# Two-layer graph network on one core: drains for own-semaphore waits, index loads for two bodies at a time, four places for edge loads

## The reference

```
h = relu(layernorm(x))
# layer 0
m    = relu(concat(h[src], edge) @ Wmsg.T + b)
m    = relu(m @ Wmsg2.T + b2)
mean = segment_sum(m, dst) / count
x    = x + concat(h, mean) @ Wapply.T + b
# layer 1
h     = relu(layernorm(x))
alpha = softmax of edge_weight over the edges of one dst
agg   = normalise(segment_sum(alpha * h[src], dst))
comb  = normalise(0.5 * (h @ Wself + b + agg @ Wnb + b))
out   = x + layernorm(comb) * gamma + beta
```

## Time and profile before

| | us |
|---|---|
| median of three runs | 10865.57 |
| the profiled execution | 10872.07 |
| its span in the trace | 10870.3 |
| POOL busy | 6155.9 (57%) |
| PE busy | 5331.9 (49%) |
| DVE busy | 3580.0 (33%) |
| ACT busy | 1136.7 (10%) |

### The profile page before, as it was taken

The page is one execution under the profiler, slowest core; times in us unless marked ns, Lnnn a source line. Parts: engine busy times, 40 slices in busy tenths (PEclk is TensorE's granted clock), DMA queues, the critical chain, the costliest instruction groups (busy, mean ns, idle before and its releaser), DMA issues.

```text
span 10870.3 us, 94616 instructions
## 1 busy us (share of the span) xinstructions
PE 5331.9 (49%) x26549; PEld 4117.8 (38%) x26549; DVE 3580.0 (33%) x14159; ACT 1136.7 (10%) x2108; POOL 6155.9 (57%) x6486
## 2 busy tenths in 40 slices
PE   4666666666655555566666533332333233233334
PEld 3444444444444344344444423222222222222224
DVE  4333233323222222222222433333333333333336
ACT  2111111111111111111111200000000000000002
POOL 4555555555554444455555466666666666666663
PEclk7777777777777677777777655655555555555556
DMA  4222222222222222222222222221111111111112
GB/s 151 56 57 54 56 56 55 57 58 57 61 67 56 57 57 59 58 55 56 58 56 57 65 57 56 56 55 49 46 46 47 46 46 47 46 46 47 46 47 72
DMA packets 412673, 618.83 MB, mean 57 GB/s; under 512 B 171795, under 2 KB 274175, under 8 KB 411263
## 3 DMA queue, kind: packets, MB, share of 16 engines
q0 software_dynamic: 206336, 422.99, 15.0%
q1 hardware_dynamic: 192624, 183.30, 6.1%
q10 hardware_dynamic: 13200, 6.56, 0.2%
HBM read 576.45 MB, written 35.92 MB: 56 GB/s over the span
## 4 chain that ended last, share of the span: by engine, by line
another core or an unknown queue 49%; PE 25%; issue 12%; DVE 12%; ACT 1%; DVEq 1%; DMA 0%; SPq 0%; POOL 0%; ACTq 0%; POOLq 0%
PE bank L1056 13%; DVE acc L884 7%; PE bank L1118 6%; PE bank L1115 3%; PE bank L1053 2%; DVE onehot L887 1%; DVE work L887 1%; ACT work L581 1%; DVEq L866 1%; DVEq L884 0%; DVE xq L711 0%; DVE acc L711 0%; DVE acc L995 0%; ACT work L587 0%
## 5 line engine op out<-in xcount | busy, mean ns | idle before, releaser
L493 POOL DMA_INDIRECT rows_ring<-p_table,idx x3224 | 3087.5, 958 | 2951.8 <-DMA idx<-in_src_ring 1790.9
L884 DVE TENSOR_TENSOR acc<-acc,bank 128x128 f32 x6448 | 1826.0, 283 | 7192.7 <-remote 5639.5
L493 POOL DMA_INDIRECT rows_ring<-h_table,idx x3224 | 3052.5, 947 | 1635.2 <-issue 1013.2
L887 DVE TENSOR_SCALAR onehot<-iota,dloc,coef 128x128 f32<-128x128 f32 x4840 | 1703.6, 355 | 16.5 <-ACT coef L558 13.3
L1056 PE MATMUL bank<-work,rows_ring 128*128 128x128 f32 x3216 | 694.6, 370 | 1867.6 <-DVE work L887 665.6
L1056 PE MATMUL bank<-onehot,work 128*128 128x128 f32 x6448 | 1094.4, 325 | 863.4 <-issue 676.4
L1056 PE MATMUL bank<-onehot,rows_ring 128*128 128x128 f32 x3232 | 743.8, 401 | 1247.1 <-remote 594.9
L1056 PEld LDWEIGHTS bank<-work,rows_ring 128*128 128x128 f32 x3216 | 597.9, 270 | 1968.7 <-issue 1911.4
L1056 PEld LDWEIGHTS bank<-onehot,work 128*128 128x128 f32 x6448 | 1002.8, 237 | 898.9 <-issue 711.3
L1056 PEld LDWEIGHTS bank<-onehot,rows_ring 128*128 128x128 f32 x3232 | 651.6, 297 | 1323.7 <-issue 1261.4
L1118 PE MATMUL bank<-work,we_sb 64*128 64x512 f32 x1612 | 1045.4, 724 | 164.7 <-issue 164.1
(11 more groups left out here) (121 smaller groups left out, 1066.1 us busy)
## 6 DMA issues: line engine op xcount, KB each, us to landing
work<-in_edge_t SPq DMA_DIRECT2D x403, 256.0 KB
rows_ring<-p_table,idx POOLq DMA_INDIRECT x3224
rows_ring<-h_table,idx POOLq DMA_INDIRECT x3224
idx<-in_src_ring SPq DMA_DIRECT2D x404, 8.0 KB
ht_rows<-rows_ring SPq DMA_DIRECT2D x25, 256.0 KB, 2.3
p_table<-rows_ring SPq DMA_DIRECT2D x25, 256.0 KB, 2.5
work<-ht_rows SPq DMA_DIRECT2D x25, 256.0 KB
h_table<-work ACTq DMA_DIRECT2D x25, 256.0 KB
```

The costliest lines, as they stand in the source:

```text
L493: pool.indirect_dma_start(out=rows_ring[:, 16 * h + G * k + j, :], out_offset=None, in_=table[:, :], in_offset=bass.IndirectOffsetOnAxis(a ...
L884: dve.tensor_tensor(win, win, ps_sum[layer][k % slots][:, j * P:(j + 1) * P], ALU.add).then_inc(added, 1)
L887: ins = dve.tensor_scalar(hot_slots[layer][k % slots][:, j * P:(j + 1) * P], iota[:, :], dloc[:, ds(t, 1)], coef[:, ds(t, 1)], ALU.is_equa ...
```

## The change

1. **Drains.** `Order` is gone. `link` is now a `dve.drain()` behind the instruction; in `tail_step` the marks become drains, on ACT too. Before each addition into `acc` stands a drain in place of the wait at L882, and the semaphore of the sums is raised once a group, at its fourth addition, in place of four times. PE's and ACT's waits on it count groups (`FINAL` is rounded up to groups).
2. **Indices.** `idx` holds two pairs of bodies, 64 tiles each. A load brings 64 tiles, 102 loads in all in place of 404. In layer 0, SP loads the pair for bodies i+2 and i+3 when PE has done the m1t steps of bodies up to i-1; in layer 1 alike. POOL waits for indices once in two bodies.
3. **Edges.** `ef_ring` has four places, on both halves of the partitions (`we_sb` is held twice to match). The load of a chunk waits for the group six before its first. `load_pre` comes at the end of a body's loads.

```
-                        if later(gs * G + j):
-                            dve.wait_ge(added, gs * G + j)
+                        dve.drain()
                         win = acc[:, ds(at[j], P)]
-                        dve.tensor_tensor(win, win, ps_sum[layer][k % slots][:, j * P:(j + 1) * P], ALU.add).then_inc(added, 1)
+                        total = dve.tensor_tensor(win, win, ps_sum[layer][k % slots][:, j * P:(j + 1) * P], ALU.add)
...
+                if adds:
+                    total.then_inc(added, 1)
...
-                for h in range(2):
-                    if h and beside is not None:
-                        load_pre(beside)
-                    half = 2 * i + h
-                    if later(i):
-                        load_idx(0, half, h, i)
-                    for c in range(2):
-                        chunk = 2 * half + c
...
-                        if later(chunk, 2):
-                            sp.wait_ge(S["m1t_in_psum"], 2 * chunk - 2)
+                for chunk in range(4 * i, min(4 * i + 4, -(-NG // 2))):
+                    if chunk >= 4:
+                        sp.wait_ge(S["m1t_in_psum"], 2 * chunk - 6)
+                    sp.dma_start(ef_ring[chunk % 4], edge_t[chunk, :, :]).then_inc(S2["edges_loaded"][chunk % 4], 16)
+                if i >= 2 and i % 2 == 0 and i // 2 + 1 < NPAIR:
+                    sp.wait_ge(S["m1t_in_psum"], 8 * i)
+                    load_idx(0, i // 2 + 1)
+                if beside is not None:
+                    load_pre(beside)
...
+            def next_idx(i):
+                if i >= 2 and i % 2 == 0 and i // 2 + 1 < NPAIR:
+                    sp.wait_ge(S["sums1_in_psum"], 8 * i)
+                    load_idx(1, i // 2 + 1)
...
+                if i % 2 == 0:
+                    pool.wait_ge(s_idx[layer][turn], 16 * (pair // 2) + 16)
                 for h in range(2):
-
-                    pool.wait_ge(s_idx[layer][h], 16 * i + 16)
...
-            order = Order(dve, S["vector_order"])
-            link = order.link
+
+            def link(ins):
+
+                dve.drain()
```

More of the change, by code:

```diff
@@ L45 @@
 PARTS = 8
-FINAL = [min(T, (E - N + (c + 1) * G * P - 1) // P + 1) for c in range(NBATCH)]
-X1_AT = -(-FINAL[0] // G) + 3
+FINAL = [-(-min(T, (E - N + (c + 1) * G * P - 1) // P + 1) // G) for c in range(NBATCH)]
+X1_AT = FINAL[0] + 3
 LAST_BODIES = X1_AT // 8
@@ L146, in gnn @@
         wgt = work[:, 10 * 512:10 * 512 + LEN]
-        ef_ring, m1t_sb, m2_sb = work[0:DE, 0:2048], place[6:8], place[8:10]
+        m1t_sb, m2_sb = place[6:8], place[8:10]
+        ef_ring = [work[DE * (n // 2):DE * (n // 2) + DE, 1024 * (n % 2):1024 * (n % 2) + 1024] for n in range(4)]
         ring4 = [rows_ring[:, 4 * n:4 * n + 4, :] for n in range(6)]
@@ L346, in stage_scalars, with load_idx @@
                 sp.dma_start(stage[0:T - whole * P, whole, :], coef_flat[n][whole * P * P:EP].rearrange("(t e) -> t e", e=P)).then_inc(S["scalars_staged"], 16)
[L348 to L351, removed]
+            def load_idx(layer, pair):
+                h = (pair + layer) % 2
+                sp.dma_start(idx[:, h, :], src_ring[pair, :, :]).then_inc(s_idx[layer][h], 16)
             def loads0(i):
@@ L385, in load_soft @@
                 sp.dma_start(wgt, weight_flat.rearrange("(p l) -> p l", p=P)).then_inc(S["soft_in_loaded"], 16)
-            for h in range(2):
-                load_idx(0, h, h)
+            for pair in range(2):
+                load_idx(0, pair)
             store_scalars(0)
@@ L420, in beside1 @@
                     sp.dma_start(table_rows(self_rows, c - 2), four(self_out[h])).then_inc(S2["self_stored"][h], 16)
-                if later(c):
-                    for half in range(2):
-                        load_idx(1, 2 * c + half, half, c)
+                next_idx(c)
             for c in range(NBATCH + 2):
@@ L447, in _ @@
                 load_self(c)
[L448 to L455, removed]
+            for i in range(NBATCH + 2, NPOOL):
+                next_idx(i)
+            ahead = 14
+            for c in range(4, ahead):
+                load_self(c)
             for c in range(NBATCH):
@@ L970, in tail_step @@
                 if inv is not None:
-                    order.after(marks["inv"])
-                    marks["inv"] = order.mark(dve.reciprocal(root, root))
+                    dve.drain()
+                    dve.reciprocal(root, root)
                 if raw is not None:
@@ L998, in tail_step @@
                 if raw is not None:
-                    order.after(marks["r2"])
-                    marks["v"] = order.mark(dve.tensor_tensor(v, v, both_parts, ALU.add))
+                    dve.drain()
+                    dve.tensor_tensor(v, v, both_parts, ALU.add)
                 stats = batch_at(3)
@@ L1005, in tail_step @@
                         ins = dve.bn_stats(stat6[:, at, :], acc[:, at * P:(at + 1) * P])
-                    marks["stats", stats] = order.mark(ins)
                 if raw is not None:
-                    order.after(marks["v"])
+                    dve.drain()
                     dve.tensor_tensor(r2, r2, v, ALU.add).then_inc(S["unit_arg_ready"], 1)
@@ L1018, in tail_step @@
                 if scl is not None:
-                    order.after(marks["scale"])
+                    dve.drain()
                     dve.scalar_tensor_tensor(mu_s, mu_s, -0.5, scale, ALU.mult, ALU.mult).then_inc(S["scale2_ready"], 1)
```

100 lines of the change are left out of this document (39 added, 61 removed).

## The result

The changed kernel takes 9967.99 us, the median of four runs (9965.93 to 9970.64), the kernel before on the same chip 10860.9 (10851.8 to 10873.19). The ratio is 0.9177, 95% interval 0.9161 to 0.9193. That is 893 us less, where 1,080 were forecast. The profiled run took 9969.66, its span is 9968.0.

The account below looks back on a forecast made before the run. No engine alone bounds the kernel: layer 0's cycle closes on POOL's index wait, layer 1 on pauses from late messages. 91 + 4833 + 63 + 4679 + 97 + 25 = 9788 us span, forecast 9780, range 9000 to 10400.

Parts of the forecast that it names:

- 38 + 80: Layer 0: 38 us for 25 bodies with `load_pre`, plus 80 us for slow first body, vector steps and closing steps.
- 27.3 - 4.0 = 23.3 or 23.4 us a half: Layer 0's half body without the index wait: 46.8 us a body, so 4833 us for the layer, 1117 less.
- layer 1 stands at 46.3 beside it: Reason for taking 46.8 us a body in layer 0: layer 1, without index wait to speak of, takes 46.3.
- The 0.14 us a gather: Cost of each POOL gather beyond its 1.25 us, paid in a pause however runs are cut; some 0.14 us.
- What is late next: In layer 0, after the index wait goes, the release of held messages itself: the pause after each POOL run.
- 46 to 48 us a body: Sign to look for: layer 0's pace after the change, with layer 1 within 1 us of 46.3.
- 0.60 us a tile: DVE's additions with drains: 0.60 us a tile, 0.14 more for 6448 tiles, some 900 us, nearly all hidden.
- None 2 us apart within a group: Sign to look for: DVE's additions 0.55 to 0.65 us apart, none 2 us apart within a group.
- There DVE sets the pace: The 97 us behind the last gather: DVE's step is 6.27 us, and drains add 25 us there.
- PE and ACT become the pace: Rival for layer 0: held messages cost its groups more, 51.5 us a body, 10250 us in all; chance 17%.
- The messages are the scarce thing: Rival: fewer messages from DVE's additions shorten the hold, 42 us a body in both layers, 8860 us; chance 14%.
- Slower by constant hold: Rival: POOL never stops for indices, messages are held nearly always, 62 us a body in layer 0, 11170 us; chance 5%.

Follow-up runs that it names:

- e4b_indices_only: Kernel before with own-semaphore waits, index loads by pairs of bodies and `load_pre` at the end of a body's loads, two edge places: ratio 0.9083.
- e1b_own_waits: Changed kernel with its drains taken back to own-semaphore waits, index loads by pairs and four edge places kept, where messages are held: 9814.1 us.
- h3_wider_memsets: `e1b_own_waits` with a wait once a group and a 64-partition by 384-byte memset on POOL behind each gather: 10274.76 us, ratio 0.9429.
- the first set: Drains, indices, edges each alone, and the change without drains, against the kernel before (8323.65 us), nothing held: 8370.36, 8313.54, 8314.2, 8312.38 us.
- h1_slower_gathers: `e1b_own_waits` edits with a POOL drain and one-column memset behind each gather, against the kernel before: 22067.03 us, ratio 2.0259.

## Why the prediction was right, and where it was off

**The bound, and the indices: right.** Layer 0 had the prize, POOL's index wait was what a cycle waited for last, and no wait on `idx` is left. The indices alone carry it, as `e4b_indices_only` shows (with `load_pre` moved); the edges, which the step put together with them, add nothing that can be seen beside them. Layer 0's time beyond median body times 100.75 is 5012 - 4896 = 116 us, forecast 38 + 80 = 118; that is partly luck, for the 38 us of `load_pre` are not in it. Its 25 bodies take 48.9 us in the mean, those behind them 48.7, so some 6 us in all.

**Layer 0's pace: the mis-sized term.** Forecast 46.8 us a body, measured 48.6, and 1.8 x 100.75 = 181 us is nearly all of the 180 us by which the span is longer than forecast (9968 against 9788). The term is "27.3 - 4.0 = 23.3 or 23.4 us a half": two runs of 16 gathers in a body, each with a pause of 3.3 us beyond the pitch, 0.21 us a gather. What the runs show in its place:

- The base was too low. 4.0 us were taken from one cycle of 27.3 us, 54.6 a body, while the prediction itself has 56.1 for the plain stretch. The same saving from 56.1 gives 48.1.
- The drains are in it: 44 us of the layer (4967 against 4923 us on one chip), 0.44 us a body in the mean. 48.1 + 0.44 comes near 48.6; the agreement is arithmetic, no proof, since the cycle has changed its form.
- The restart was too short. The earlier trace rows gives 9119.84 - 9119.19 = 0.65 us and not 0.4, and after the change the median from the first engine's restart to POOL's is 0.77 us.
- The form is another: 374 pauses, 3.7 a body, of 2.6 us each beyond the pitch. Together they are 975 / 3224 = 0.30 us a gather in layer 0 (0.27 in `e1b_own_waits`), against 0.19 in layer 1 (0.18).

The check "layer 1 stands at 46.3 beside it" misled. The 0.14 us a gather came from one run in each layer, and layer 0's toll after the change is larger than layer 1's. Why it is larger, no run shows. Between two chips the changed kernel's layer 0 differs by 45 us too (5012 and 4967).

**What is late next: right in kind.** Pauses of 3.20 and 5.57 us in the rows above (the longest 8.4), put down to "remote" and to PE, took the place of the index wait, as forecast. The sign "46 to 48 us a body" was missed by 0.6. `h3_wider_memsets` shows that the hold depends on the rate of gathers; by what it comes is open.

**The drain: wrong in size, and in its effect beside a long run of gathers.** 0.60 us a tile was taken, nearest to the lower bound; 0.70 was measured, since an addition starts 0.16 us after the drained one-hot, not 0.06. Most of it was hidden, as said: of 0.24 x 3224 = 774 us of DVE time a layer, 44 show in layer 0 and 2 in layer 1. The layers' sums had 0 and 10. "None 2 us apart within a group" was wrong: such additions went from 2.1 or 2.8 to 2.8 us, because each step of DVE's queue takes 0.70 us there, not only its message. The rule that was weighed (the Trainium skill, "VectorE: DVE Perf Modes", "Rules for kernel authors": keep down the number of instructions, not of semaphores) had no gain from the drains, and the runs agree: they lose 0.6% to 1.5%. The forecast's own 35 us of loss was too little as well; 77 were measured beside the other parts.

**Layer 1, end and gap.** 4650 against 4679: the index waits of 93 us, counted at nothing, gave 29 us at most. The end is 130 us against 122, and `e1b_own_waits` has 98, so the +25 for drains is +32 (41 where nothing is held). "There DVE sets the pace" leaves something out: of the 98 us of `e1b_own_waits` 32 go with the holds, for the same kernel has 66 where nothing is held. The 63 us between the layers became 83, which the forecast had as unchanged; `e1b_own_waits` has 77 and `e4b_indices_only` 72, so drains make some 6 of them. The rest goes with the early indices, but by what link wasn't tried.

**The rivals.** "PE and ACT become the pace" wanted 51.5 us a body and got 48.6. "The messages are the scarce thing" finds no support: with three own messages fewer for each group, layer 1 stays at 4622 us against 4620, on the same chip. The drains come with it, so a small gain that they eat up isn't excluded. "Slower by constant hold" did not come: the stop of the ring frees the queue as said against it. All of this holds for chips or occasions with holds. Where there are none, by the first set the parts bring 0.1% or cost 0.6%; the changed kernel as a whole didn't run there.

## What to carry to other kernels

When one engine's wait goes, look at what a second wait in the same cycle already costs and at the pace of a stretch that never had the first one; here that stretch's toll was too low (0.19 us a gather, where 0.30 came). Take a saving off the mean of the whole stretch, not off one cycle that reads well. Before two edits in one queue are priced apart, ask whether they free the same instruction; here edges gave 5% alone and nothing more beside the indices. Where an independent instruction stands between two dependent ones, a wait on one's own message (0.46 us a tile here) is cheaper than a drain (0.70), which waits for that instruction too; and where queue steps stretch to 0.70 us, the drain saved nothing either. Look at how many semaphore records a trace has before you build on a wait that it can't name.

## What the hardware showed that was not expected

- In every set but the first, gathers back to back go with late messages between the other engines. At a pitch of 1.25 us DVE stands 11.36 and 13.52 us before an addition with no named releaser; at 1.55 us and at 3.3 us no such wait is seen. The toll in layer 1 is 0.18 to 0.21 us a gather in eight traces. In the first set the same pitch has no hold at all.
- With drains, some 700 of the 6448 queue steps of the additions take 0.70 us where messages are held; with own waits none is longer than 0.1 us, and without holds none with drains either.
- While messages are late, the gathered rows are not: a gather's last packet ends 1.25 us after POOL's instruction, with holds and without.
- The same kernel took 8323.65 us in one set and 10771 to 10895 in five others, a factor of 1.3, with no step between. It isn't settled whether this is the chip or the occasion: a later set on a chip of the same number (that of `h1_slower_gathers`) had the kernel before at 10893.01.
- A drain of POOL behind a gather delays the next instruction by 1.69 us, and with the memset the pitch grows from 1.25 to 3.3 us. A memset of one column (0.12 us) behind a gather is free; one of 384 bytes a partition takes 0.44 us, and 0.30 us of it show.
